# Second block of the first layer's convolution: 25 rounds a group from rows in a new order, with copied tiles made by ScalarE and VectorE

## The reference

```
def _denoise_block(x, w1, b1, w2, b2, w3, b3, a, b, c):
    trip = _triplets(x)              # each channel with its two neighbours: T sets of 3
    ...
    o = a * _conv_reflect(xf, w1, b1, 1, 2) + b * _conv_reflect(xf, w2, b2, 2, 4) + c * _conv_reflect(xf, w3, b3, 4, 8)
    return jnp.tanh(o).reshape(B, T, H, W)
y = _denoise_block(x, blk1_w1, ...)
z = _denoise_block(y, blk2_w1, ...)
...
x = x + _L0_conv_ref(_gn(x), ...)    # then three more layers
```

## Time and profile before

| | us |
|---|---|
| three runs | 5301.88, 5305.83, 5305.98 (median 5305.83) |
| the profiled execution, own time | 5308.6 |
| its span in the trace | 5306.8 |
| its mean granted TensorE clock | 0.985 |

### The profile page before, as it was taken

The page is one execution under the profiler, slowest core; times in us unless marked ns, Lnnn a source line. Parts: engine busy times, 40 slices in busy tenths (PEclk is TensorE's granted clock), DMA queues, the critical chain, the costliest instruction groups (busy, mean ns, idle before and its releaser), DMA issues. The chain is left out here.

```text
span 5306.8 us, 178754 instructions
## 1 busy us (share of the span) xinstructions
PE 4988.3 (94%) x78653; PEld 2961.4 (56%) x78653; DVE 3369.1 (63%) x6195; ACT 2400.5 (45%) x2999; POOL 1366.5 (26%) x1629
## 2 busy tenths in 40 slices
PE   4999999999999999999999988998777899999998
PEld 2444444444444467777777763433655466666665
DVE  5653453453433555555555547887999688888888
ACT  2222231231221111111111118875999699999997
POOL 0000000000002111111111100001777255555556
PEclk9999999999999999999999999999999999999999
DMA  8777777777766667667676659997887365666554
GB/s 247 241 250 232 236 252 228 237 251 231 233 206 221 206 207 233 209 206 233 207 224 216 207 161 320 326 320 247 307 309 292 120 152 149 152 152 152 150 152 120
DMA packets 366866, 1166.79 MB, mean 220 GB/s; under 512 B 60458, under 2 KB 61097, under 8 KB 287019
## 3 DMA queue, kind: packets, MB, share of 16 engines
q1 hardware_dynamic: 363928, 1152.98, 68.7%
q10 hardware_dynamic: 2162, 2.39, 0.2%
HBM read 683.58 MB, written 453.51 MB: 214 GB/s over the span
## 5 line engine op out<-in xcount | busy, mean ns | idle before, releaser
L682 PE MATMUL c_p<-c_w,wc 128*32 128x512 f16 x55296 | 3017.4, 380 | 25.5 <-DMA c_w<-xs 23.6
L682 PEld LDWEIGHTS c_p<-c_w,wc 128*32 128x32 f16 x55296 | 1761.9, 97 | 1252.5 <-issue 30.4
L742 ACT ACTIVATE c_t<-c_p,cbias,cscale 128x512 f32<-128x512 f32 x512 | 398.4, 778 | 2385.8 <-PE c_p L682 2385.7
L607 DVE TENSOR_TENSOR a_x<-c_t,a_x 128x512 f32<-128x512 f32 x256 | 222.1, 868 | 656.9 <-ACT c_t L742 656.9
L597 DVE TENSOR_SCALAR c_y<-c_t 128x512 f16<-128x512 f32 x256 | 109.4, 427 | 704.1 <-ACT c_t L742 586.9
L1705 PE MATMUL f_P<-f_qh,f_wt 64*64 64x512 f16 x4608 | 545.7, 378 | 1.8 <-DVE f_t L1601 1.8
L1705 PE MATMUL f_P<-f_hl,f_wt 64*64 64x512 f16 x4608 | 545.3, 379 | 0.0
L1866 POOL TENSOR_TENSOR f_y<-f_y,f_x 128x512 f32<-128x512 f32 x256 | 331.1, 1293 | 448.0 <-DVE f_hl L1580 442.0
L1601 DVE SCALAR_TENSOR_TENSOR f_t<-f_P,f_kk,f_ci 128x256 f32<-128x256 f32 x1024 | 423.6, 476 | 11.9 <-PE f_P L1705 7.2
L813 POOL COPY c_y<-c_y 128x16 f16<-128x16 f16 x512 | 87.2, 200 | 1278.0 <-DVE c_y L599 1278.0
L1465 POOL TENSOR_TENSOR e_hl<-e_g,e_hl 128x2048 f16<-128x2048 f32 x63 | 257.2, 4083 | 609.5 <-ACT e_hl L1415 609.5
(11 more groups left out here) (263 smaller groups left out, 5896.5 us busy)
## 6 DMA issues: line engine op xcount, KB each, us to landing
c_w<-xs SPq DMA_DIRECT2D x576, 264.0 KB, 7.8
c_w<-ys SPq DMA_DIRECT2D x576, 264.0 KB, 3.9
d_x<-x SPq DMA_DIRECT2D x128, 1024.0 KB, 7.6
x<-d_x SPq DMA_DIRECT2D x128, 1024.0 KB, 5.1
ys<-c_y SPq DMA_DIRECT2D x576, 132.0 KB
xs<-a_hl SPq DMA_DIRECT2D x70, 1056.0 KB, 11.3
a_x<-in_x SPq DMA_DIRECT2D x256, 256.0 KB, 5.6
a_x<-in_x SPq DMA_DIRECT2D x128, 512.0 KB, 5.0
```

The lines of the kernel that those rows point to most:

```text
L607: v.tensor_tensor(xw[:, g, :], tl[:, :], xw[:, g, :], ALU.add).then_inc(c_lo, 1)
L682: t = p.matmul(pg[32 * j:32 * j + 32, :], wu[:, blk, wl, var, di, :], buf[:, bk, xl * PW + PAD + dx:xl * PW + PAD + dx + NW], start=(di == ...
L742: s.activation(tt_[n % 3][:, :], pp[:, n % 4, :], ACT.Tanh, bias=cbias[:, blk:blk + 1], scale=cscale[:, blk:blk + 1]).then_inc(c_act, 1)
```

## The change

In block 2 alone, the 32 rows of a window are laid down so that the 24 rows that column offsets -2, -1, 1 and 2 need are partitions 0 to 95, and the 8 outer rows are 96 to 127. The weights of block 2 are moved to the same order (`wc2`, by 24 small DMAs during units 8 to 19). For those four column offsets:

- weight low x value high stays as it was: 4 rounds;
- a tile `near` (`c_n`), made by two VectorE copies, holds the high rows of the 96 inner partitions and, in its last 32, the low rows of partitions 64 to 95: 4 rounds;
- a tile `twice` (`c_2`), made by two ScalarE copies, holds the low rows of partitions 0 to 63 two times, the second time shifted by three columns, so that one round serves offsets -2 and 1 and the next -1 and 2: 2 rounds.

The other five column offsets keep 15 rounds, so a group of block 2 is 15 + 4 + 4 + 2 = 25 rounds, and the weights for the two tiles are `wn2`, filled by twelve GpSimd copies in units 30 and 31. The copies for group n + 1 stand in front of the eviction (ScalarE) and of the sum (VectorE) of group n; they wait for the window and until TensorE is done with group n - 1, which read the same buffer of two. Window loads of block 2 come for two groups at once, as four DMAs of 32, 16, 8 and 8 partitions of 16.5 KB in place of four of 32 pieces of 8.25 KB. Block 1 keeps its 27 rounds in another order, with the norm's small matmuls at the same place as before, after 15 rounds.

```diff
-        wc = [sb(ctx, f"wc{i}", [128, 2, 2, 3, 9, 32], F16) for i in range(2)]
+        wc = [sb(ctx, f"wc{i}", [128, n, 2, 3, 9, 32], F16) for i, n in enumerate((2, 1))]
+        wall = [sb(ctx, f"w_2{i}", [128, 2304], F16) for i in range(2)]
+        wc2 = [w[:, 0:1728].rearrange("p (b v d c) -> p b v d c", b=2, v=3, d=9) for w in wall]
+        wn2 = [w[:, 1728:2304].rearrange("p (v e c) -> p v e c", v=3, e=6) for w in wall]
...
+        near = [sb(ctx, f"c_n{i}", [128, 4, PW], F16) for i in range(2)]
+        twice = [sb(ctx, f"c_2{i}", [128, 4, PW], F16) for i in range(2)]
...
+        def doubled(n):
+
+            return 4 * NU <= n < 8 * NU
...
+        def four_rows(e, n):
+
+            u, g = divmod(n, 4)
+            rows_in(e, u, g)
+            e.wait_ge(c_pe, n - 1)
+            return win[u % 2][:, 4 * g:4 * g + 4]
...
+                def copies(n):
+                    w = four_rows(v, n)
+                    v.tensor_copy(near[n % 2][0:96], w[0:96, :, 0:PW]).then_inc(c_nh, 1)
+                    v.tensor_copy(near[n % 2][96:128], w[64:96, :, PW:RW]).then_inc(c_nl, 1)
...
+                        if doubled(4 * u + g + 1):
+                            copies(4 * u + g + 1)
...
-                    pg, buf, wu = pp[:, n % 4, :], win[half], wc[pr % 2]
-                    p.wait_ge(c_ld[half][g], n_win(u))
+                    pg, buf, wu = pp[:, n % 4, :], win[half], wc2[pr % 2] if blk else wc[pr % 2][:, 0]
+                    rows_in(p, u, g)
                     if (u, g) == (2, 0):
                         p.wait_ge(w_sw, 32)
+                    if (u, g) == (NU, 0):
+                        p.wait_ge(w_s2, 16 * 24)
+                        p.wait_ge(w_wn, 12)
                     if n >= 4:
                         p.wait_ge(c_act, n - 3)
-                    for di, dx in enumerate(DX):
-                        for z, (wl, xl) in enumerate(((0, 0), (0, 1), (1, 0))):
-                            for j in range(4):
-                                bk = 4 * g + j
-                                var = 0 if (half, bk) == (0, 0) else (2 if (half, bk) == (1, 15) else 1)
-                                t = p.matmul(
-                                    pg[32 * j:32 * j + 32, :], wu[:, blk, wl, var, di, :],
-                                    buf[:, bk, xl * PW + PAD + dx:xl * PW + PAD + dx + NW],
-                                    start=(di == 0 and z == 0), stop=(di == 8 and z == 2), tile_position=(0, 32 * j))
...
+                    def four(weights, source, at, start=False, stop=False):
+                        for j in range(4):
+                            bk = 4 * g + j
+                            var = 0 if (half, bk) == (0, 0) else (2 if (half, bk) == (1, 15) else 1)
+                            t = p.matmul(pg[32 * j:32 * j + 32, :], weights[:, var], source[:, j, at:at + NW],
+                                         start=start, stop=stop, tile_position=(0, 32 * j))
+                        return t
+
+                    rows4 = buf[:, 4 * g:4 * g + 4]
+                    for di in (4, 0, 1, 7, 8):
+                        for wl, xl in ((0, 0), (0, 1), (1, 0)):
+                            four(wu[:, wl, :, di], rows4, xl * PW + PAD + DX[di], start=(di, wl, xl) == (4, 0, 0))
...
+                    for di in (2, 3, 5, 6):
+                        t = four(wu[:, 1, :, di], rows4, PAD + DX[di])
+                    if not blk:
+                        for di in (2, 3, 5, 6):
+                            for xl in range(2):
+                                t = four(wu[:, 0, :, di], rows4, xl * PW + PAD + DX[di], stop=(di, xl) == (6, 1))
+                    if blk:
+                        p.wait_ge(c_nh, n_copied(n))
+                        p.wait_ge(c_nl, n_copied(n))
+                        for e, di in enumerate((2, 3, 5, 6)):
+                            four(wn2[pr % 2][:, :, e], near[n % 2], PAD + DX[di])
+                        p.wait_ge(c_2a, n_copied(n))
+                        p.wait_ge(c_2b, n_copied(n))
+                        four(wn2[pr % 2][:, :, 4], twice[n % 2], PAD - 2)
+                        t = four(wn2[pr % 2][:, :, 5], twice[n % 2], PAD - 1, stop=True)
...
+                def copies(n):
+                    w = four_rows(s, n)
+                    s.activation(twice[n % 2][64:128, :, PAD - 2:PAD - 1 + NW], w[0:64, :, PW + PAD + 1:PW + PAD + 2 + NW], ACT.Copy).then_inc(c_2b, 1)
+                    s.activation(twice[n % 2][0:64, :, PAD - 2:PAD - 1 + NW], w[0:64, :, PW + PAD - 2:PW + PAD - 1 + NW], ACT.Copy).then_inc(c_2a, 1)
...
+                        if doubled(4 * u + g + 1):
+                            copies(4 * u + g + 1)
...
+                def near_weights(i):
+
+                    hi, to = wc2[i][:, 0], wn2[i]
+                    for z, (rows, of, e, d) in enumerate(((slice(0, 96), slice(0, 96), 0, 2), (slice(0, 96), slice(0, 96), 2, 5),
+                                                          (slice(96, 128), slice(64, 96), 0, 2), (slice(96, 128), slice(64, 96), 2, 5),
+                                                          (slice(0, 64), slice(0, 64), 4, 2), (slice(64, 128), slice(0, 64), 4, 5))):
+                        q.tensor_copy(to[rows, :, e:e + 2], hi[of, :, d:d + 2]).then_inc(w_wn, 1)
+                        q.wait_ge(w_wn, 6 * i + z + 1)
...
-                    if u >= 2:
+                    if blk:
+                        e.wait_ge(c_pe, 4 * (u - 2) + g + 2)
+                    elif u >= 2:
                         e.wait_ge(c_pe, 4 * (u - 2) + g + 1)
...
                     for gp in (0, 1) if p == 0 else (p + 1,):
+                        at = pair(b, gp, 0, 16 * half + 4 * g)
+                        if blk:
+                            for first, count, off in ((0, 32, 0), (80, 16, RW), (64, 8, 12 * VP - RW), (112, 8, 8 * VP - RW)):
+                                e.dma_start(win[half][first + gp % 2:first + 2 * count:2, 4 * g:4 * g + 8].rearrange("p k w -> p (k w)"),
+                                            dram(src, at + off, [[CP, count], [1, 8 * RW]])).then_inc(c_ld[half][g], 16)
+                            continue
...
+                        if u + 2 < NU and not late:
                             load(u + 2, g)
+                        if NU <= u + 2 < 2 * NU and g % 2:
+                            load(u + 2, g - 1)
+                        if 8 <= u < 20 and g == 2:
+                            for i, new, old, count in outer_rows()[2 * u - 16:2 * u - 14]:
+                                e.dma_start(wall[i][new:new + 2 * count - 1:2, 0:1728],
+                                            wc[0][old:old + 8 * count - 7:8, 1].rearrange("p b v d c -> p (b v d c)")).then_inc(w_s2, 16)
```

More of the change, by code:

```diff
@@ L344, in layer0 @@
         c_pe, c_act, c_hi, c_lo, c_pad, c_bn, c_mm, c_ag = (sem("c_" + n) for n in ("pe", "act", "hi", "lo", "pad", "bn", "mm", "ag"))
-        w_c, w_f, w_t, w_sel, w_hi = (sem("w_" + n) for n in ("c", "f", "t", "sel", "hi"))
+        w_c, w_f, w_t, w_sel, w_hi, w_wn, w_s2 = (sem("w_" + n) for n in ("c", "f", "t", "sel", "hi", "wn", "s2"))
+        c_nh, c_nl, c_2a, c_2b = (sem("c_" + n) for n in ("nh", "nl", "2a", "2b"))
         w_td = [sem(f"w_td{i}") for i in range(2)]
@@ L383, in n_ys, with n_win, rows_in, n_copied @@
             return 16 * sum(8 + 4 * (place(r)[2] in (0, 7)) for r in range(u % 2, u, 2))
-        def n_win(u):
-            return 32 * sum(1 + (place(r)[2] == 0) for r in range(u % 2, u + 1, 2))
+        def n_win(u, g):
+            return sum((1 + (place(r)[2] == 0)) * (64 * (g % 2 == 0) if place(r)[0] else 32) for r in range(u % 2, u + 1, 2))
+        def rows_in(e, u, g):
+            if place(u)[0]:
+                g = g // 2 * 2
+            e.wait_ge(c_ld[u % 2][g], n_win(u, g))
+        def doubled(n):
+            return 4 * NU <= n < 8 * NU
+        def n_copied(n):
+            return n - 4 * NU + 1
+        def four_rows(e, n):
[3 more added lines that the diff above has]
+            return win[u % 2][:, 4 * g:4 * g + 4]
+        def outer_rows():
+            out = []
+            for new, old, n in ((0, 0, 16), (32, 6, 16), (64, 66, 8), (80, 4, 8), (96, 68, 8), (112, 2, 8)):
+                out += [(new + q, old + q, n) for q in range(2)]
+            return [(i, new, old + (1 - 2 * (old % 2)) * i, n) for i in range(2) for new, old, n in out]
         def table_of(u):
@@ new lines, in products @@
+                    rows4 = buf[:, 4 * g:4 * g + 4]
+                    for di in (4, 0, 1, 7, 8):
+                        for wl, xl in ((0, 0), (0, 1), (1, 0)):
+                            four(wu[:, wl, :, di], rows4, xl * PW + PAD + DX[di], start=(di, wl, xl) == (4, 0, 0))
+                    i, s = stage_of(n - 1)
+                    if s == 0:
+                        p0(i)
+                    if s == 1:
+                        p1_(i)
+                    for di in (2, 3, 5, 6):
+                        t = four(wu[:, 1, :, di], rows4, PAD + DX[di])
```

(16 more changed lines are left out.)

6 lines of the change are left out of this document (removed).

## The result

| | before | changed | forecast |
|---|---|---|---|
| median of the runs, us | 5305.00 | 5215.62 (5213.77 to 5224.65) | 5197 (5190 to 5257) |
| profiled execution, us | 5308.6 | 5213.77 | 5198 |

The ratio is 0.9836, with a 95% interval from 0.9819 to 0.9853: faster, by 89.4 us between the medians. The sum of the prediction gave 110.6, and with the 2 us for late windows 108.6. Some 19 us were given back.

The account below looks back on a forecast made before the run. Block 2 was taken as bound by TensorE's number of matmuls: 8 fewer at 54.0 ns in 256 groups save 110.6 us, so 5305.8 - 110.6 = 5195, plus 2 for late windows: 5197 us, range 5190 to 5257.

Parts of the forecast that it names:

- a part given back: Outcome band of 5203 to 5295 us, by rival 1 or the mild form of rival 2; chance 0.24.
- What bounds block 2, and what is removed: Block 2 is bound by the number of matmuls; 8 of 108 removed in each of 256 groups save 110.6 us.
- VectorE's copies: Two copies a group in block 2, about 0.70 us each; VectorE then occupied 4.70 of 5.40 us.
- rival 2: VectorE becomes block 2's bound, 5295 or 5825 us, chance 0.04; mild form: GpSimd and VectorE hold each other up, 5279.
- ScalarE's copies: Two copies a group in block 2, 1.915 us each; with tanh 4.61 of 5.40 us, 0.8 idle, no table reload.
- rival 3: ScalarE needs two table loads a group in block 2: 7.2 us a group, +345, 5650 us; chance 0.01.
- I add 2 us for windows that come late where an image begins: Term for twice the window loads at image starts in block 2, taking 5195 to 5197 us.
- That is free: In block 2 the busier eight DMA engines need 4.5 of 5.40 us a group, so the DMAs cost nothing.
- rival 1's partial form: Window DMAs partly collide, 5.5 us a group or stalls at three image starts: 10 to 60 us back, 5207 to 5257.
- a margin of 4.0 us: VectorE's copies for the next group in block 2 end at 5.5 us, TensorE wants them at 9.5.
- rival 1: Window DMAs into SBUF halves collide, stretched by f: 2.1 + 2.40 f us a group, at most 5579; slower, chance 0.06.
- Block 1: Keeps 27 rounds and its time; its reordering, the 24 early small DMAs and twelve GpSimd copies cost nothing nameable.

Follow-up runs that it names:

- nodouble: The changed kernel with only one of the window's two channel groups loaded at the start of images 2 to 4 in block 2; 5203.8 us, ratio 0.9801.
- four1: The changed kernel with four buffers for x instead of two, x asked for at the old place, one unit ahead; 5228.4 us, ratio 0.9867.
- combfour1: The changed kernel with the edits of comb and four1 together; 5198.3 us, ratio 0.9813.
- comb: The changed kernel with window rows in steps of three, six and four, five DMAs for four, weights moved to match; 5197.0 us, ratio 0.9808.
- fourspread: The changed kernel with the edits of four and spread together; 5210.9 us, ratio 0.9817.
- even16: The changed kernel with the upper half's window DMAs (16, 8 and 8 partitions) made into two of 16; 5218.6 us, ratio 0.9841.
- spread: The changed kernel with a pair's window as two DMAs of 32 partitions in steps of four over all 128; 5207.4 us, ratio 0.9821.
- res1: The changed kernel with SP asking for x one group later in each unit; 5244.4 us, ratio 0.9894.
- four: The changed kernel with four buffers for x instead of two, x asked for two units ahead; 5230.1 us, ratio 0.9854.

## Why the prediction was right, and where it was off

5215.6 lies in the stated range of 5190 to 5257, but not in the band that I thought most likely (5189 to 5203, chance 0.62). It lies in the band of "a part given back", which had 0.24. The mechanism of the gain was right, the loss beside it underrated.

**What bounds block 2, and what is removed: right.** The 37 groups that lost 0.2 us in all run at the forecast pace, 100 matmuls of 54 ns. 110.1 us were there to be had in 255 steps, 91.6 came.

**VectorE's copies: right within 0.13 us.** 0.81 and 0.72 us against 0.70 each. VectorE is occupied 5.43 - 0.80 = 4.63 us a group, 4.70 was forecast. The mild form of rival 2, GpSimd and VectorE in each other's way, is visible and harmless: the copies of the 96 partitions take 0.81 on average, GpSimd's product 1.24 us where it took 1.055. The rule of the Trainium skill (page "SBUF — State Buffer", "Who interferes with whom") agrees with that, for the copies too. One figure of that rival doesn't come out: 4.70 and 1.0 make 5.70 us a group and 5271, not 5.73 and 5279; no chance hangs on it.

**ScalarE's copies: right.** 1.92 us each, 0.81 idle a group, no table load: rival 3 did not happen.

**The DMAs: the step that failed is "I add 2 us for windows that come late where an image begins".** It was the sum's only term for late transfers, and it measured 18.5. It rested on the DMA sum before it, 4.5 of 5.40 us, "That is free": the share measured was no higher, 0.81 of the mean engine, and it was not free. The range had room for it ("it takes 10 to 60 us back: 5207 to 5257"), so the result came out as rival 1's partial form. Four things were missing from that sum:

- The largest part was at a place that I did not name, the first 21 groups of block 2 (10.0 us), where block 1's last stores still fill the queues. That it was 0.1 in nodouble, with the same program there, makes part of the 18.5 a matter of the single execution or chip.
- Lateness reached TensorE by way of x too, not only of the windows: VectorE's list puts the next copies behind a sum that waits for x. I gave that path a margin of 4.0 us and did not ask how late x could be. It cost 5.6 us.
- TensorE stood 5.7 us for "issue". That cost 9.0 us, the largest part by cause, and no term had it.
- The clock: a stall of 2.45 us cost 4.3 (it is within the costs above, 3.4 us in all).

That the placement of the windows sets the loss is shown by four1 and combfour1 (row order alone, one chip: 30 us), with comb and fourspread pointing the same way; that it isn't the pieces of 8, by even16. What isn't shown is that the halves of SBUF are the reason, as rival 1 has it. Its size by the Trainium skill, page "SBUF — State Buffer", section "Door 1: The DMA port swizzle (why `[64,N]` ≈ `[32,N]`)", an estimate of 6.1 us a group, did not come: 5.47 was measured. If the rest took 2.1 us a group as forecast, the windows take 0.794 x 5.43 - 2.1 = 2.2 us on the mean engine in the changed kernel and 0.704 x 5.42 - 2.1 = 1.7 in comb: a factor of 1.3, where the two rates that this page of the Trainium skill gives make 1.67. The direction agrees; the size doesn't, and the measurement decides. And spread, each of whose DMAs reaches over all 128 partitions, takes 0.777 x 5.43 - 2.1 = 2.1 by the same sum, hardly less than the changed kernel. So halves alone don't tell comb from spread. (0.794, 0.704 and 0.777 are the data queue's shares in the DMA views of 1800 to 3000 us.)

Nor did rival 1 act as its formula has it. Against the 1.92 us forecast for the windows on the mean engine, 2.2 is a factor of 1.15, far below the 1.38 at which the engines would set the pace. The loss came as single late transfers.

**Block 1: right.** The early DMAs and GpSimd's copies show nowhere; block 2 starts 2.6 us earlier.

What stays open: what the stalls for "issue" are (that instructions queue behind data is argued from shares, and from their going away in comb), which property of comb's row order lowers the share, why the first 21 groups lose 10 us in one execution and nothing in another of the same program, and why four1 has a higher share than the changed kernel with the same bytes.

## What to carry to other kernels

When a change reorders the partitions of a tile, look at where each DMA's destination then lies, and try a second order: four loads placed in one half of SBUF each took about 1.3 times the engine time of the same loads combed over it in steps of three, six and four, and it showed more at stores that landed late, at x and in TensorE's "issue" stalls than at the loads. Which order is good has to be measured; steps of four over all 128 partitions were not as good here. Price a transfer's lateness along every list that it can block: here the longest stall went x, sum, copies, TensorE, and no request moved forward or backward (res1, four, four1) helped as long as the queues were full. A mean share of 0.8 is not "free": look at the starts of images and blocks, where double loads and last stores meet. And before a pitch of one execution is explained, compare it where the programs are the same: 9.9 us of nodouble's 11 lay there.
